# A fused transformer layer: both attentions in halves and causal chunks, row maxima added by VectorE

## The reference

```python
x = x + attn(cond(x, cond_1024[:, None, :], ...), ...)
x = x + ffn(cond2(x, cond_1024, Wx, Wh, b), ...)
```

```python
a = xw_t + prev_h @ Wh
next_c = sigmoid(f) * prev_c + sigmoid(i) * tanh(g)
next_h = sigmoid(o) * tanh(next_c)
```

## Time and profile before

| | us |
|---|---|
| median of 3 runs | 687.82 (687.6 to 689.17) |
| profiled execution, first to last instruction | 692.0 |
| TensorE busy / weight loads | 463.2 / 318.3 |
| VectorE busy | 407.9 |
| ScalarE busy | 234.5 |
| GpSimd busy | 45.7 |

### The profile page before, as it was taken

How to read it: one execution, slowest core, us unless ns; L and a number is a source line. 1 busy time by engine, 2 the same in 40 slices (tenths; PEclk the granted TensorE clock), 3 DMA queues, 4 the chain that set the end, 5 groups by cost and what they waited for, 6 DMA issues and landing times.

```text
span 692.0 us, 13536 instructions
## 1 busy us (share of the span) xinstructions
PE 463.2 (67%) x5003; PEld 318.3 (46%) x5003; DVE 407.9 (59%) x2108; ACT 234.5 (34%) x818; POOL 45.7 (7%) x41
## 2 busy tenths in 40 slices
PE   0593799104839979888899889737367367367346
PEld 0231433102616756665566567536256246256334
DVE  6458533896674865767766775654444544544443
ACT  0023787232333523333433432223222232222222
POOL 9500002530000000000000000000000000000000
PEclk9997799655959985999985995555555555555555
DMA  7100200000002000000000000000000000000000
GB/s 188 45 0 0 61 2 2 0 0 0 1 0 32 1 1 2 1 3 1 2 1 3 1 2 1 2 1 1 5 6 2 5 6 1 5 5 3 5 1 5
DMA packets 9312, 7.00 MB, mean 10 GB/s; under 512 B 1845, under 2 KB 8093, under 8 KB 9246
## 3 DMA queue, kind: packets, MB, share of 16 engines
q1 hardware_dynamic: 8206, 5.60, 3.5%
q10 hardware_dynamic: 1040, 0.52, 0.3%
HBM read 4.02 MB, written 0.52 MB: 7 GB/s over the span
## 4 chain that ended last, share of the span: by engine, by line
PE 44%; DVE 36%; ACT 14%; issue 5%; DMA 1%; DVEq 0%
PE bank L1358 13%; ACT h_fac L644 6%; DVE h_off L1004 5%; PE bank L1192 5%; DVE pr L997 4%; ACT gates L642 4%; DVE gates L1001 4%; PE bank L1223 3%; PE bank L1078 3%; PE bank L1210 3%; DVE h_fac L999 2%; PE bank L1066 2%; DVE mx L916 2%; DVE q_sq L923 2%; DVE ada_b L685 2%
## 5 line engine op out<-in xcount | busy, mean ns | idle before, releaser
L1358 PE MATMUL bank<-h_off,wha 128*128 128x4 f16 x1020 | 68.3, 171 | 121.9 <-DVE h_off L1004 118.5
L1358 PEld LDWEIGHTS bank<-h_off,wha 128*128 128x128 f16 x1020 | 50.5, 106 | 166.4 <-DVE h_off L1004 160.7
L642 ACT ACTIVATE gates<-bank 128x16 f32<-128x16 f32 x256 | 46.9, 183 | 192.2 <-PE bank L1358 191.1
L997 DVE SCALAR_TENSOR_TENSOR pr<-gates 128x8 f32<-128x8 f32 x256 | 42.1, 164 | 106.3 <-ACT gates L642 106.3
L644 ACT ACTIVATE h_fac<-gates 128x4 f32<-128x4 f32 x256 | 53.1, 207 | 110.0 <-DVE gates L1001 110.0
L1004 DVE TENSOR_TENSOR h_off<-h_fac 128x4 f16<-128x4 f32 x256 | 43.3, 169 | 70.0 <-ACT h_fac L644 70.0
L1192 PE MATMUL bank<-kT,qz 128*128 128x128 f32 (+1 forms) x256 | 71.4, 394 | 0.0
L1358 PE MATMUL bank<-h_low,wha 128*128 128x4 f16 x1020 | 63.8, 167 | 0.0
L1358 PE MATMUL bank<-h_off,whb 128*128 128x4 f16 x1020 | 62.5, 166 | 0.0
L1006 DVE TENSOR_TENSOR_SCAN h_low<-h_fac,h_off 128x12 f16<-128x12 f32 x256 | 46.7, 183 | 8.7
L611 ACT ACTIVATE p_mla<-bank,mx 128x128 f32<-128x128 f32 (+1 forms) x128 | 44.4, 414 | 18.1 <-DVE mx L916 18.1
(11 more groups left out here) (224 smaller groups left out, 737.9 us busy)
## 6 DMA issues: line engine op xcount, KB each, us to landing
qz<-qz SPq DMA_DIRECT2D x16, 64.0 KB, 2.0
x_tm<-in_x ACTq DMA_DIRECT2D x1, 512.0 KB, 5.0
wf<-in_L_cond_w_f SPq DMA_DIRECT2D x2, 256.0 KB, 5.7
x_tb<-in_x SPq DMA_DIRECT2D x4, 128.0 KB, 2.7
qz<-qT SPq DMA_DIRECT2D x16, 32.0 KB
out_y<-tb SPq DMA_DIRECT2D x7, 64.0 KB, 1.9
ada_w<-in_L_cond_w_ada SPq DMA_DIRECT2D x1, 384.0 KB
bf_all<-in_L_cond_b_f SPq DMA_DIRECT2D x1, 256.0 KB, 5.8
```

Source lines behind the costliest of these rows:

```text
L642: nc.scalar.activation(gates[:, k, 0:GW], src, ACT.Tanh, scale=1.0 / A_SCALE).then_inc(gates_act, 1)
L997: V.scalar_tensor_tensor(pr[:, k, :], gates[:, k, B:3 * B], 1.0, gates[:, k, 3 * B:5 * B], ALU.add, ALU.mult).then_inc(p_ready, 1)
L1358: ins = T.matmul(acc[:, g * B:(g + 1) * B], w[:, g, :], h, start=False, stop=True, skip_group_check=True)
```

## The change

The conditional layer is run in two sides, first the queries of positions 0 to 127 of each sequence, then those of 128 to 255. `UNITS` now lists 32 units of the conditional attention by side. Its score products use 32 rows of the array per head (`tile_position`), so `q_slab`, its zeros and its transfers are gone. A generator `side(k)` on each engine carries a side through the rest of the layer, four tiles at a time, with operations of 128x4; square roots on VectorE come from the bits of the number and two polynomial steps (8 dependent operations) in place of a logarithm and an exponential on ScalarE. `until` runs a generator to a mark.

The causal attention runs in chunks of 32 positions. Chunks 0 to 3 have 4 units each and chunks 4 to 7 have 8; a unit is four heads, and 4 or 2 sequences, with 32(c+1) keys. VectorE finds the negated maxima and adds them into `p_mla`, ScalarE takes exponentials of `p_mla` in two halves, VectorE transposes each half in 32x32 blocks.

Before step 0 stand side 0 and chunk 0, and the first part of side 1. `CHUNK_FROM` places chunks 1 to 7 on the steps without input projections (28 of 32), and `Pace` with `VEC_AT`, `ACT_AT` and `PE_AT` the rest of side 1 on steps 0 to about 70: on VectorE one piece between the cell and its tanh, and two or three at the end of a step. The last `ffn` begins at step 198, a piece every 8 steps. The addition of the biases `b_ada` moves from TensorE to VectorE and the four later modulation rows come from one product of 512 columns, not four; some loads and weight preparations come earlier.

The core of the diff:

```diff
+        UNITS = [(k, g, bp, jp) for k in range(HALVES) for g in range(NG) for bp in range(2) for jp in range(2)]
+        PER_GROUP = 4
+        PER_HALF = NG * PER_GROUP
+
...
+        def unit_of(c, u):
+            if c < 4:
+                return u, (0, 1, 2, 3)
+            g, bp = divmod(u, 2)
+            return g, (2 * bp, 2 * bp + 1)
+
+        UNIT_EVERY = 3
+        SCORES_FROM = 7
+        VALUES_AFTER = 8
+
+        def values_end(c):
+            return SCORES_FROM + UNIT_EVERY * (unit_count(c) - 1) + VALUES_AFTER
+
...
+        CHUNK_FROM = {1: 0, 2: 20, 3: 40, 4: 64, 5: 88, 6: 112, 7: 136}
+
+        def attending(t):
+            i = free_of.get(t)
+            if i is not None:
+                for c, i0 in CHUNK_FROM.items():
+                    if 0 <= i - i0 < chunk_span(c):
+                        yield c, i - i0
+
+
+        VEC_AT = dict(second=0, joined=0, log1=12, log2=15, moved=25, v_ready=36, squared0=38, squared1=40, squared2=42, squared3=45,
+                      f1_factor=49, fed=53, third=60, fourth=65)
+        ACT_AT = dict(bent=11, log1=14, log2=23, moved=31, v_turned=34, up=51, third=58, fourth=64)
...
+            def go(self, t, most):
+                for _ in range(most):
+                    if t < self.at:
+                        return
+                    m = next(self.chain, "end")
+                    if m is not None:
+                        self.at = S if m == "end" else self.table[m]
 
...
+            exps(0, PER_HALF)
+            exps(16, 18)
+            first, second = side(0), side(1)
+            until(first, "turned")
+            exps(18, 19)
...
+            def m_exp(c, u, part):
+                m = unit_base(c) + u
+                g, bs = unit_of(c, u)
+                n = STEPS * (c + 1)
+                act.wait_ge(mx_ready, m + 1)
+                cols = slice(len(bs) // 2 * part * n, len(bs) // 2 * (part + 1) * n)
+                nc.scalar.activation(p_mla[:, m % 2, cols], p_mla[:, m % 2, cols], ACT.Exp).then_inc(mp_ready, 1)
...
+                def root(a, y):
+                    done(late)
+                    on(V.tensor_scalar(at(y).bitcast(I32), at(a).bitcast(I32), -0.5, ROOT_BITS, ALU.mult, ALU.add))
+                    yield
+                    done(late)
+                    on(V.tensor_tensor(at(T1), at(a), at(y), ALU.mult))
+                    yield
+                    done(late)
+                    on(V.scalar_tensor_tensor(at(T1), at(T1), -ROOT_K, at(y), ALU.mult, ALU.mult))
+                    yield
+                    done(late)
+                    on(V.scalar_tensor_tensor(at(T2), at(T1), ROOT_C, at(y), ALU.add, ALU.mult))
+                    yield
+                    done(late)
+                    on(V.tensor_tensor(at(T1), at(a), at(T2), ALU.mult))
+                    yield
+                    done(late)
+                    on(V.scalar_tensor_tensor(at(T1), at(T1), -1.0 / ROOT_S ** 2, at(T2), ALU.mult, ALU.mult))
+                    yield
+                    done(late)
+                    on(V.scalar_tensor_tensor(at(Y), at(T1), 10.0 / 3.0, at(T1), ALU.add, ALU.mult))
+                    yield
+                    done(late)
+                    on(V.scalar_tensor_tensor(at(y), at(Y), 5.0, at(T2), ALU.add, ALU.mult))
+                    yield
+
...
+            def m_max(c, u):
+                m = unit_base(c) + u
+                g, bs = unit_of(c, u)
+                n = STEPS * (c + 1)
                 vec.wait_ge(ms_mm, m + 1)
                 if m >= 2:
-                    vec.wait_ge(mp_ready, m - 1)
-                V.tensor_reduce(mx[:, m % 2, 0:512 // n], bank[:, m % 2, :].rearrange("p (j n) -> p j n", n=n), AX.X, ALU.max,
-                                negate=True).then_inc(mx_ready, 1)
-
-            def m_weights(m):
-                vec.wait_ge(mt_mm, m + 1)
+                    vec.wait_ge(mx_ready, m - 1)
+                V.tensor_reduce(mx[:, m % 2, 0:len(bs)], bank[:, 3 + m % 2, 0:len(bs) * n].rearrange("p (b n) -> p b n", n=n), AX.X, ALU.max,
+                                negate=True).then_inc(m_top, 1)
+                if m >= 2:
+                    vec.wait_ge(mt_ready, 2 * m - 2)
+                vec.wait_ge(m_top, m + 1)
+                V.tensor_tensor(p_mla[:, m % 2, 0:len(bs) * n].rearrange("p (b n) -> p b n", n=n),
+                                bank[:, 3 + m % 2, 0:len(bs) * n].rearrange("p (b n) -> p b n", n=n),
+                                mx[:, m % 2, 0:len(bs)].unsqueeze(2).to_broadcast([P, len(bs), n]), ALU.add).then_inc(mx_ready, 1)
+
+            def m_turn(c, u, part):
+                m = unit_base(c) + u
+                g, bs = unit_of(c, u)
+                n = STEPS * (c + 1) * len(bs) // 2
+                vec.wait_ge(mp_ready, 2 * m + part + 1)
                 if m >= 2:
                     vec.wait_ge(mpv_mm, m - 1)
-                V.tensor_copy(pt_mla[:, m % 2, :], bank[:, 2 + m % 2, :]).then_inc(mt_ready, 1)
-
-            def m_out(g):
-                vec.wait_ge(mpv_mm, last_unit(g) + 1)
...
             def scores(w):
-                u, pair = divmod(w, 2)
-                g, bb = divmod(u, B)
+                k, g, bp, jp = UNITS[w]
...
+                for i in range(4):
+                    bb, kc = 2 * bp + i // 2, i % 2
+                    for j in (2 * jp, 2 * jp + 1):
+                        rows = slice(SLOTS * HD * j, SLOTS * HD * (j + 1))
+                        ins = T.matmul(bank[:, 2 * (w % 2) + j % 2, i * P:(i + 1) * P], kS[rows, g, bb * S + kc * P:bb * S + (kc + 1) * P],
+                                       qS[rows, g, bb * S + k * P:bb * S + (k + 1) * P], start=True, stop=True,
+                                       tile_position=(SLOTS * HD * j, 0), skip_group_check=True)
                 ins.then_inc(score_mm, 1)
 
-
...
+            def m_scores(c, u, part):
+                m = unit_base(c) + u
+                g, bs = unit_of(c, u)
+                n = STEPS * (c + 1)
+                if part == 0:
+                    if u == 0:
+                        pe.wait_ge(mqk_ready, c + 1)
+                    if m >= 2:
+                        pe.wait_ge(mx_ready, m - 1)
+                rows = slice(32 * g, 32 * g + 32)
+                for i in range(len(bs) // 2 * part, len(bs) // 2 * (part + 1)):
+                    T.matmul(bank[:, 3 + m % 2, i * n:(i + 1) * n], qz[rows, c % 2, bs[i]].rearrange("p j t -> p (j t)"), kT[rows, bs[i], 0:n],
+                             start=(i == 0), stop=True, skip_group_check=True, tile_position=(32 * g, 0))
+                    ins = T.matmul(bank[:, 3 + m % 2, (i + 1) * n - STEPS:(i + 1) * n], sel32[rows, :], mask32[rows, :],
+                                   start=False, stop=True, skip_group_check=True, tile_position=(32 * g, 0))
+                if part:
                     ins.then_inc(ms_mm, 1)
 
...
+            def m_values(c, u):
+                m = unit_base(c) + u
+                g, bs = unit_of(c, u)
+                n = STEPS * (c + 1)
+                pe.wait_ge(mt_ready, 2 * m + 2)
+                if u == 0:
+                    pe.wait_ge(mv_ready, 2 * c + 2)
+                    if c:
+                        pe.wait_ge(moT_ready, c)
+                for kb in range(c + 1):
+                    for i, b in enumerate(bs):
+                        ins = T.matmul(bank[32 * b:32 * b + 32, 5, g * GROUP * VW:(g + 1) * GROUP * VW],
+                                       pt_mla[:, m % 2, i * n + kb * STEPS:i * n + (kb + 1) * STEPS],
+                                       vbd[:, b, kb, GROUP * g:GROUP * (g + 1), :].rearrange("p j v -> p (j v)"),
+                                       start=(kb == 0), stop=(kb == c), skip_group_check=True, tile_position=(0, 32 * b))
+                ins.then_inc(mpv_mm, 1)
+
...
+                    until(first, f"turn{g - 1}")
+                units(PER_GROUP * g + 2, PER_GROUP * (g + 1))
+            until(first, f"turn{NG - 1}")
+            units(16, 17)
+            until(first, "turned")
+            units(17, 18)
+            until(first, "projected")
+            units(18, 31)
+            until(first, "v_turned")
+            until(first, "up1")
+            units(31, 32)
+            until(second, "turn0")
+            until(first, "up3")
+            until(second, "turn1")
+            until(first, "normed")
+            until(first, "end")
+            until(second, "turn3")
+            until(second, "turned")
+            until(second, "projected")
```

## The result

The changed kernel takes 667.99 us, median of 4 runs (666.36 to 669.96), where the kernel before has 688.5 (687.6 to 690.32): a ratio of 0.9689, with a 95% interval of 0.966 to 0.9718. I had forecast 638.2. The direction was right and the time lies inside my range of 608 to 672, but only 20.5 us of a forecast 50 came. The kernel before has two groups of times, and these four runs of it all lie in the longer one; against the shorter, around 677, the change brings 9 us ("The kernel before, again").

The account below looks back on a forecast made before the run. Bound by when step 0 can start plus a 407 us chain that nothing shortens: step 0 at 160.4, steps 407.2, jobs 66.6, tail 8.2 make 642.4, less 4.2 is 638.2 us; range 608 to 672.

Parts of the forecast that it names:

- Before the attention: Start to first eviction of queries, keys and values: 27.1 us instead of 53.71, including 3.0 for waits on GpSimd.
- 16 units at 1.45: Side 0's attention: 16 units at 1.45 us each, 24.0 with the first scores, bounds 18 and 34.
- Rival B: TensorE's paired tiles don't run side by side in 128-column units: 2.1 a unit, 652 us in all; chance 0.14.
- Side 0's chain: From side 0's attention to its condition output: terms of 72.4 less 7.4 overlap, 65 us, bounds 60 to 78.
- Chunk 0: From side 0's chain to step 0, first causal chunk and start: 15.3 us, bounds 12 to 20.
- Steps: Jobs inside the recurrence's steps cost 66.6 us beyond 407.2 of plain steps, bounds 40 and 100.
- Rival E: A 32x32 transposition on VectorE costs four times a copy, making the kernel slower: 699 us; chance 0.02.
- Side 1's pieces: Rest of side 1 inside the steps: 9.3 us on VectorE, 8 for TensorE's products plus scores.
- Rival C: Handovers are dearer, as waiting pieces of side 1 or units hold the gates: +32, 670 us; chance 0.11.
- rival D: Jobs inside the steps hide better than counted: jobs at 40, 612 us; chance 0.11.
- The offset: From profiled span to median time: 4.2 us taken off, since the earlier profile had 692.0 against a median of 687.82.

Follow-up runs that it names:

- The kernel before, again: The kernel before, run unchanged twice more for further profiles: 689.86 and 675.54 us.
- e_pool_late: Changed kernel with one added wait: GpSimd's masks and gate-bias split begin only after the attention's first exponential; 659.66 us.
- e_side0_alone: Changed kernel reordered so that side 1's attention runs after side 0's chain on every engine, not inside it; 699.85 us, one run.
- e_chunk0_mix: Changed kernel with side 1's first VectorE pieces put between chunk 0's pieces and ScalarE's matching squares four places later; 667.54 us.
- after: The changed kernel itself, as profiled after the change; 667.99 us.
- e_up_first: Changed kernel with side 1's last first-half attention unit, its exponential and copy moved behind side 0's first feed-forward products; 668.4 us.
- e_starts: Changed kernel with chunks 5, 6 and 7 starting 1, 2 and 3 free steps later and the last feed-forward every 7th step; 666.0 us.
- e_turn_later: Changed kernel with the second half's transposition of each unit moved one step later; 657.76 us.
- e_fill_steps: Changed kernel plus one extra f16 TensorE product of 512 columns a step in steps 80 to 191; 680.32 us.
- e_filled: Changed kernel plus extra f16 TensorE products of 512 columns ahead of step 0, including chunk 0; 678.0 us.

## Why the prediction came out as it did

**Before the attention: right.** 53.7 became 28.4 (27.1). The 13.67 of the earlier trace rows did go. I had added 3.0 for waits on GpSimd. Behind the statistics they were 1.57, 1.71 and 1.71, each for one GpSimd operation, where such an operation takes 0.17 to 0.20 by itself: 4.4 in all, and `e_pool_late`, without them, is 4.2 earlier. (One of 3.00 lies ahead of the statistics, which wait for their input anyway.) The sum was off by 1.3 only. The Trainium skill (SBUF — State Buffer, "Who interferes with whom") speaks of a lock for one instruction. These waits of the changed kernel agree with that; 13.97 in the longer run of the kernel before does not, and there the measurement decides. So the long wait was a matter of chance, and I priced it as certain: right for the runs of the longer group, 13 too much for the others.

**16 units at 1.45: mis-sized, 28.1 for 24.0.** At the higher clock a group of four takes 6.12, 1.53 each: near. The first three units came 2.39, 2.39 and 1.87 apart, at 1.2 GHz for the first two and part of the third: 2.3 together beyond my price, and I had taken the higher clock throughout. Rival B, tiles that do not overlap, would have needed 2.1 throughout; it falls.

**Side 0's chain: the step that failed.** 65 stood for 73.4, the largest part of the 29.8 by which the forecast was too low. The term in it that was too small is the feed-forward: 13 in my sum, 22.7 from v_ready to the bias. The two ends on VectorE in the changed kernel, and between them TensorE's products:

```profile
123.13 0.76 DVE L1169 TENSOR_TENSOR v_tm<-v_tm,sm 128x256 f32<-128x256 f32 x2
...
127.19 3.78 PE L1449 MATMUL bank<-vT,wf 128*128 128x512 f32 x4 [0.75 <-ACT vT L644]
...
130.90 1.07 PE L1401 MATMUL bank<-q_sq,vaug 128*32 128x128 f32 x16
...
133.84 1.98 PE L1449 MATMUL bank<-vT,wf 128*128 128x512 f32 x4 [0.93 <-ACT k_pair L652]
...
136.76 3.73 PE L1455 MATMUL bank<-ones,q_pair 128*128 128x1 f32 x32 [0.49 <-ACT k_pair L652]
...
140.35 5.45 PE L1463 MATMUL bank<-wf,k_pair 128*128 128x128 f32 x32
...
145.84 1.13 DVE L1189 SCALAR_TENSOR_TENSOR ta<-bank,sm,bf 128x128 f32<-128x128 f32 x4 [3.37 <-PE bank L1463]
```

Three causes can be read. The sums of squares take 3.73 at a granted clock of 1.00 (136.7 to 140.5); I had no term for them beside 2 for the norms. Two products of 512 columns took 3.78 at 0.51 granted (127.2 to 131.0) where the next two took 1.98, and the second product 5.45 at 0.69 where I had 3.6. And a unit of side 1 stands between them on TensorE: I had side 1's attention hidden in the first 30 us of the chain, but its last exponential starts at 127.0, 41 us in. I had given 2 to the lower clock and 2 to side 1's work in the way. The latter is 5 to 7 (`e_side0_alone`), 4.4 of it in the feed-forward; how the rest splits between the missing term and the clock was not tested. My upper bound of 78 did hold the 73.4.

**Chunk 0: mis-sized, 19.3 for 15.3.** The terms as I wrote them add up to 16.7 even with three units at 1.0, so 1.4 of the 4.0 is a wrong addition. I had put VectorE in front. In its place stand TensorE's products at 1.2 GHz: the four score products of a unit, with their masks, take 1.9, and the order on VectorE changes nothing (`e_chunk0_mix`).

**Steps: 73.8 for 66.6; VectorE's part right, TensorE's too small.** The stalls that I computed for chunks 4 to 7 were 0.56, 0.73, 0.90 and 1.07 to a unit; measured are 0.61, 0.78, 0.94 and 1.11. (My figures hold 0.11 that the formula does not give; the rows of the long step show it, the addition starting 0.11 after the reduction's end.) The transposition was taken at a copy's price, 0.28 for 128 columns. 96 of them have a mean of 0.37; 64 columns take 0.24 and 256 take 0.43, so a further column costs the 0.001 that it costs a copy. Rival E, four times a copy, falls; the Trainium skill (Vector Engine (DVE) Microarchitecture Reference, "The reshape front-end and per-opcode configuration"), with one element per cycle and lane, agrees with these rows.

Side 1's pieces cost 15.9 where I had 9.3 and 8. With them left out, the steps behind a reduction exceed plain ones by 30.7 (34.8 in my sum), and all other steps by 27.3, where my sum has 14.5 left: 12 of TensorE (20 less side 1's 8), 1 and 1.5. That is where the 7.3 come from. Twelve steps from 102 to 171, at the starts of chunks 5, 6 and 7, are 12.0 longer than plain ones in the changed kernel. There value projections share a step with value products, or the value products wait for a copy on ScalarE, as in step 171, which takes 2.87:

```profile
513.29 1.18 PE L1499 MATMUL bank<-vbd,pt_mla 128*32 128x36 f32 x32 [1.28 <-ACT qS L728]
```

I had 7 for all value projections and 5 for overlaps. Rival C, handovers dearer by 32, and rival D, 27 less, are both refuted by 481.1.

**The offset: wrong.** I took 4.2 off because the profiled run before was above its median. The changed kernel's profiled run was near its own: 668.2 of span against 667.99. In every run here the time is 1.7 to 1.9 above the span of the same execution; the 4.2 were a mark of that one profile, whose steps take 423.2 where two more profiles of the kernel before show 418.5 and 418.0.

**What I should have drawn from my own numbers.** I wrote that the addition shares one step in three with a reduction and a transposition, and that 0.60 is free in each. Of the two other steps one held no job of the unit on VectorE and one a single transposition. The cost that I put at 34.8 is one of placement, and 22.9 us go by moving the same instructions.

## What to carry to other kernels

Inside a chain with fixed slack an operation costs what its step's queue exceeds the slack by, not its own duration: here the same instructions cost 22.9 us less when they are spread over three steps, as much as leaving the addition out brings (22.5), so spread jobs over the steps before weighing one engine against another. Give every group of TensorE's products a term, and price them in a stage with many handovers at its lower clock, from rows of that clock. And look at more than one profile of the kernel before: a long wait seen once may be a chance, and what the change brings then depends on which run it is held against.

## What the runs showed of the hardware

- A VectorE operation on 1x128 that met 16 GpSimd writes back to back took 1.43 in one profile and 13.67 and 13.97, until the last write's end, in two others of the same kernel.
- With the same code, TensorE's granted clock over 4 us at the start of the attention was 0.50, 0.72, 0.81, 0.84 or 1.00 (`after`, `e_up_first`, `e_starts`, `e_turn_later`, `e_fill_steps`). Step 0 lies up to 4.3 apart in these runs.
- In chunk 0 added f16 products of 128 rows raised the granted clock from 0.50 to 0.80. One such product a step left steps 80 to 191 at 0.54 to 0.57, where the changed kernel has 0.51 to 0.52.
- A score product of 32 rows and 32 columns in f32, with the bf16 product that adds its mask, comes every 0.50 at 1.2 GHz and every 0.27 in `e_filled`. A product of 128 rows and 128 columns takes 0.51 (8 instructions in 2.05, two to a product). A sixteenth of the work costs as much.
